# Degree products of a round in four lots of six instead of one lot of 24, and the degree copy behind the last eviction

## The chip, the cores and the metric

The kernel runs on one core of one Trainium2 chip. The metric is the device time of one execution in microseconds; the kernel before takes 1332.59 us (median of 3 runs, 1330.99 to 1334.54). The profile is of one more execution, which took 1327.6 us.

## The reference, cut to what matters

Four graph layers (a three-hop light convolution, a weighted convolution, a mean aggregation, a message network) run one after the other over the same graph of 3125 nodes and 53125 edges, sorted by destination. What the change touches is computed once, ahead of the first layer:

```
# adjacency counts, as a dense matrix
A[s, d] = number of edges from s to d
# first layer and third layer: plain in-degree; second layer: sum of the edge weights + 1
deg  = segment_sum(ones, dst)
deg1 = segment_sum(edge_weight, dst) + 1
x0   = relu(layernorm(x)) * rsqrt(deg)      # what the first product with A takes in
```

## The kernel before, in words

The nodes are cut into 25 chunks of 128 (`NC`), the edges into 416 tiles of 128, taken two at a time as 208 pairs (`PAIRS`). Because the edges are sorted, all edges of a pair end in a window of 20 neighbouring nodes (`PW`). The first stage, the build, makes the matrix `A` (128 x 25 x 3144, half precision) window by window. It has 26 rounds (`ITB`) of 8 pairs (`PS`), and five engines take part, each in its own loop over the rounds, tied by semaphores alone:

- VectorE (`window_hots`, lines 2094 to 2115) makes one-hot tiles: two lane tiles and two small ones a round (`same_as`, L2091) and two tiles for each pair (L2108). Behind pair 2 of a round it makes `hot_d`, 768 wide (L2114), the one-hot of the destinations in a chunk, once GpSimd has made `rel` and once TensorE has used the `hot_d` of the round before (`hot_d_used`).
- TensorE (`windows`) makes a window from two matmuls of 300 or 400 columns (L1552) and one of 25 columns for the edge of the pair (L1557), into one of four PSUM banks of `big`. It may not begin pair k before ScalarE has evicted pair k-4 (`window_kept`).
- ScalarE (`keep_windows`) evicts each window into `A` at a place that it reads from a register (L1345, `A[:, :, bass.ds(bases[k], PW)]`). Each eviction waits for the one before it, as windows overlap. The eight places of a round are loaded from SBUF into registers at its start (`load_nodes`, L1341, whose instruction is at L1024).
- From round 1 on TensorE also makes the degrees of one chunk of 128 nodes: 24 products of 4 columns with 32 columns of weights each (L1566), six for each of four groups of 32 nodes (`SUBS` = 4, `KS` = 6), into bank 0 of `seg`. They stand behind pair 5 (`k == PS - 3`). ScalarE copies the result, 128 x 4, into `deg` behind the eviction of pair 6 (L1349, `k == PS - 2`).
- GpSimd (`chunk_distance`) makes `rel` (L1266) and, once `hot_d_used` has come, copies the four pieces of `w_near` (L1270), which the products of the next round read.

When all 25 chunks have their degrees, VectorE waits for the last copy (`deg_kept`) and works through some twenty short instructions (from L2134) to the first piece of the first layer's input; TensorE then begins the products with `A` (L1628). SyncE starts the reload of `x` and the spill of a part of `A` after the last eviction.

Of the kernel before, what the change touches and what calls it, by code (L numbers as in the profile page):

```python
# [40 lines left out]
PS = 8  # L41
# [6 lines left out]
SUB, KS = 32, 6  # L48
SUBS = P // SUB
# [712 lines left out]
def dense_path(nc, sem, base_row, pair_row, x, src, dst, edge_attr, edge_weight, w1, b1, w2s, w2n, mw1, mb1, mw2, mb2,  # L762
# [3 lines left out]
    with ExitStack() as ctx:  # L766
# [117 lines left out]
        hot_d = cur_h[:, 0:SUB * KD].rearrange("p (v k) -> p v k", k=KD)  # L884
        iota_d = cur_h[:, SUB * KD:2 * SUB * KD].rearrange("p (v u k) -> p v u k", u=SUBS, k=KS)
        w_near = cur_h[:, 2 * SUB * KD:2 * SUB * KD + 4 * KD].bitcast(BF16).rearrange("p (t v) -> p t v", v=4)
# [79 lines left out]
        seg = ctx.enter_context(nc.psum_tensor("seg", [P, 4, 512], F32))  # L966
# [11 lines left out]
        hot_d_ready, hot_d_used = sem("hot_d_ready"), sem("hot_d_used")  # L978
# [22 lines left out]
        ev = sem  # L1001
# [21 lines left out]
        def load_nodes(eng, row, at, n, top):  # L1023
            _, v = nc.values_load_multi_w_load_instructions(  # L1024
                row[0:1, bass.ds(at, n)], engines=[eng.engine], min_val=0, max_val=top,
                skip_runtime_bounds_check_because="node or tile numbers, bounded where they were made")
            return v
# [291 lines left out]
        def on_scalar(act):  # L1319
# [20 lines left out]
            def keep_windows(it, degrees):  # L1340
                bases = load_nodes(act, pair_row, it * PS, PS, N - 1)  # L1341
                for k in range(PS):
                    act.wait_ge(window_built, it * PS + (PS + 1 + k))
                    act.wait_ge(window_kept, it * PS + (k + 4))
                    nc.scalar.copy(A[:, :, bass.ds(bases[k], PW)],  # L1345
                                   big[:, k % 4, 0:PC].rearrange("p (s d) -> p s d", d=PW)).then_inc(window_kept, 1)
                    if degrees and k == PS - 2:
                        act.wait_ge(hot_d_used, it)
                        nc.scalar.copy(deg[:, bass.ds(it - 1, 1), :], seg[:, 0:1, 0:4]).then_inc(ev("deg_kept"), 1)  # L1349

            keep_windows(0, False)
            with act.Fori(1, ITB) as it:
                keep_windows(it, True)
# [139 lines left out]
        def on_tensor(pe):  # L1493
# [23 lines left out]
            for c in range(4):  # L1517
                op = nc.tensor.matmul(banks[7][0:1, P:P + THR], ones[:, :], below[:, c * THR:(c + 1) * THR], start=(c == 0), stop=(c == 3))
            op.then_inc(ev("counts_ps"), 1)
            turn_rows0(4, drel_t, "drel_t")  # L1520
            for c in range(4):
                op = nc.tensor.transpose(banks[6][:, c * P:(c + 1) * P], raw_w[:, c * P:(c + 1) * P], ident[:, :])
# [8 lines left out]
            def pair_window(k):  # L1531

                return big[:, k % 4, 0:PC].rearrange("p (s d) -> p s d", d=PW)
# [5 lines left out]
            def pair_hots(slot, j):  # L1539

                at = NC * FIRST * j
                return hot_r[slot][:, at:at + NC * (SUBWIN[j][1] - SUBWIN[j][0])].rearrange("p (s d) -> p s d", s=NC)

            def windows(it, degrees, odd, first=False):
                for k in range(PS):
                    h = 2 * odd + k // 4
                    if k % 4 == 0:
                        pe.wait_ge(lanes_ready, it * 2 + (k // 4 + 1))
                    pe.wait_ge(hot_r_ready, it * PS + (k + 1))
                    pe.wait_ge(window_kept, it * PS + (k + 1))  # L1550
                    for j, (low, high) in enumerate(SUBWIN):
                        op = nc.tensor.matmul(pair_window(k)[:, :, low:high], hot_l[h][:, :, (2 * k + j) % 8],  # L1552
                                              pair_hots(k % 4 if first else k, j),
                                              start=(j == 0), stop=True, skip_group_check=(j == 1))
                    if k or not first:
                        last = (4 * odd * 4 + 2 * k - 1) % 32
                        op = nc.tensor.matmul(pair_window(k)[:, :, 0], hot_l[last // 8][:, :, last % 8],  # L1557
                                              hot_b[h][:, :, k % 4], start=False, stop=True, skip_group_check=True)
                    op.then_inc(window_built, 1)
                    if degrees and k == PS - 3:  # L1560
                        pe.wait_ge(hot_d_ready, it)
                        pe.wait_ge(ev("w_near_ready"), it * SUBS)
                        pe.wait_ge(ev("deg_kept"), it - 1)
                        for u in range(SUBS):
                            for t in range(u * KS, (u + 1) * KS):
                                op = nc.tensor.matmul(seg[u * SUB:(u + 1) * SUB, 0, 0:4], hot_d[:, :, t], w_near[:, t, :],  # L1566
                                                      start=(t == u * KS), stop=(t == (u + 1) * KS - 1))
                        op.then_inc(hot_d_used, 1)

            windows(0, False, 0, True)  # L1570
            windows(1, True, 1)
            with pe.Fori(1, ITB // 2) as two:
                windows(two * 2, True, 0)
                windows(two * 2 + 1, True, 1)
# [65 lines left out]
            for k in range(ROUNDS):  # L1640
                if k >= 2:
                    pe.wait_ge(ev("conv1_t"), k - 1)
                for c in range(4 * k, min(4 * k + 4, NC)):
                    op = nc.tensor.transpose(seg[0:D, k % 2, (c % 4) * P:(c % 4 + 1) * P], cur[:, c, :], ident[:, :])
# [79 lines left out]
            for half, ks in enumerate((range(0, 3), range(3, ROUNDS))):  # L1724
                pe.wait_ge(ev("h_L3"), half + 1)
                for k in ks:
                    if k >= 4:
                        pe.wait_ge(ev("h_t_L3"), k - 3)
                    for c in range(4 * k, min(4 * k + 4, NC)):
                        op = nc.tensor.transpose(seg[:, k % 4, (c % 4) * P:(c % 4 + 1) * P], h_nb[:, c, :], ident[:, :])  # L1730
                    op.then_inc(ev("h_ps_L3"), 1)
                for k in ks:
# [5 lines left out]
                    for c in range(4 * k, min(4 * k + 4, NC)):  # L1738
                        op = nc.tensor.matmul(big[:, k % 4, (c % 4) * HID:(c % 4 + 1) * HID], h_t[:, c * P:(c + 1) * P], mw1_r, start=True, stop=True)
# [95 lines left out]
            for c in range(4):  # L1835
                op = nc.tensor.matmul(big[:, 0, c * D:(c + 1) * D], y1_t[:, c * P:(c + 1) * P], nw2_sb, start=True, stop=True)
# [686 lines left out]
```

## Time and profile before

| what | us |
|---|---|
| median of 3 runs | 1332.59 |
| the profiled execution | 1327.6 |
| its span (first to last instruction) | 1325.8 |
| TensorE busy / VectorE / ScalarE / GpSimd, of the span | 1006.6 / 830.9 / 452.6 / 592.2 |
| ScalarE evictions of windows (L1345), 208 | 125.4 |
| mean granted TensorE clock, share of full speed | 0.862 |

The build lies between about 25 and 199 us, slices 1 to 6 of the 40 in the page's table; there the granted clock is 0.6 to 0.8 of full speed in tenths (`PEclk 9677778...`). A time in a row is counted from the start of the span. "[0.16 <-X]" behind a row is idle time of the engine ahead of it, and what by the profile ended it; that name is the last event before the start, which need not be what was really waited for. Engine names with a q (ACTq) are the sequencer of that engine, which decodes and hands over; PEld is TensorE's weight load.

### The profile page before, as it was taken

To read this page: it belongs to the slowest core of one execution; us is meant where nothing else is said; L and a number is where in the kernel's file an instruction comes from. 1 tells how busy PE (TensorE), PEld (TensorE's weight loads), DVE (VectorE), ACT (ScalarE), POOL (GpSimd) and SP (SyncE) were. 2 spreads that over 40 slices of the span, in tenths; PEclk is the share of its full clock that TensorE was granted. 3 is DMA by queue.
4 is the path that set the end of the run, shared out by engine and by line. 5 is a ranking of instruction groups with operands and counts; after the bars stand their busy time and mean duration, and the time that the engine had idled before them with its cause. 6 is when DMAs were issued, how large, how long until landed. Compare 5 with 4: busy or idle time off the path is not lost.

```text
span 1325.8 us, 24512 instructions
## 1 busy us (share of the span) xinstructions
PE 1006.6 (76%) x6145; PEld 618.1 (47%) x6145; DVE 830.9 (63%) x2605; ACT 452.6 (34%) x1035; POOL 592.2 (45%) x763
## 2 busy tenths in 40 slices
PE   3788887996667767667696787777787878777685
PEld 2566553553444545445355444434444534444443
DVE  8988877357645556757657554565555555555556
ACT  3677771011434333334013232232232323222232
POOL 6533330000665666654003656555555555555550
PEclk9677778998887788877797899999888998999997
DMA  2000006001111111100523533333333333333331
GB/s 54 2 0 0 0 0 243 1 1 22 24 23 19 20 21 22 21 19 17 168 63 75 138 81 79 76 76 76 77 73 77 75 71 77 75 73 78 72 75 34
DMA packets 145110, 72.80 MB, mean 55 GB/s; under 512 B 111917, under 2 KB 136698, under 8 KB 144922
## 3 DMA queue, kind: packets, MB, share of 16 engines
q1 hardware_dynamic: 127224, 54.98, 16.0%
q0 software_dynamic: 16448, 16.88, 6.9%
q8 instruction: 30, 0.49, 0.2%
q10 hardware_dynamic: 1378, 0.22, 0.1%
q14 instruction: 30, 0.25, 0.1%
HBM read 59.66 MB, written 12.35 MB: 54 GB/s over the span
## 4 chain that ended last, share of the span: by engine, by line
PE 41%; another core or an unknown queue 20%; issue 16%; DVE 12%; ACT 6%; DVEq 2%; POOL 1%; ACTq 1%; DMA 1%; SPq 1%; POOLq 0%
PE seg L1628 10%; PE big L1658 5%; PE big L1552 4%; PE seg L1683 4%; PE seg L1755 3%; PE big L1791 3%; PE seg L1802 2%; ACT A L1345 2%; PE seg L1566 2%; PE big L1781 1%; ACT A L1466 1%; PE seg L1696 1%; ACT A L1472 1%; PE seg L1823 1%
## 5 line engine op out<-in xcount | busy, mean ns | idle before, releaser
L1221 POOL DMA_INDIRECT A<-table,idx x338 | 327.3, 968 | 260.6 <-ACT idx L1317 154.2
L1221 POOL DMA_INDIRECT pair<-table,idx x176 | 176.2, 1001 | 126.8 <-ACT idx L1317 65.0
L1755 PE MATMUL seg<-A 128*128 128x384 f16 (+1 forms) x624 | 137.6, 370 | 44.5 <-issue 19.1
L1466 ACT COPY A<-big 128x512 f32<-128x512 f32 x104 | 61.1, 587 | 249.7 <-remote 156.7
L1345 ACT CAST A<-big 128x500 f32 x208 | 125.4, 603 | 48.0 <-PE big L1557 25.9
L1791 PE MATMUL big<-A 128*128 128x512 f32 x208 | 114.1, 631 | 33.6 <-ACT A L1466 28.3
L2033 DVE COPY A<-seg 128x512 f32<-128x512 f32 x52 | 36.0, 691 | 162.3 <-remote 150.6
L1683 PE MATMUL seg<-A,cur 128*64 128x160 f32 x750 | 94.8, 353 | 46.0 <-issue 45.9
L1397 ACT COPY A<-big 128x500 f32<-128x500 f32 x120 | 66.5, 576 | 181.4 <-remote 113.8
L1755 PEld LDWEIGHTS seg<-A 128*128 128x128 f16 x624 | 60.3, 106 | 140.5 <-issue 91.0
L1658 PE MATMUL big<-A 128*128 128x300 bf16 x480 | 106.1, 367 | 18.8 <-issue 10.4
L1472 ACT ACTIVATE A<-big,A 128x512 f32<-128x512 f32 x104 | 72.1, 694 | 139.0 <-remote 115.5
L1802 PE MATMUL seg<-A 128*64 128x512 f32 x208 | 63.2, 687 | 50.2 <-ACT A L1472 40.6
L1916 DVE TENSOR_SCALAR A<-iota_r,acc_mem,A 128x300 bf16<-128x300 f16 x240 | 74.3, 370 | 39.6 <-remote 32.3
L1683 PEld LDWEIGHTS seg<-A,cur 128*64 128x64 f32 x750 | 61.7, 158 | 75.0 <-issue 71.5
L1628 PE MATMUL seg<-A,acc_mem 128*128 128x512 f16 (+1 forms) x406 | 84.4, 363 | 7.7 <-DVEq L2146 7.7
L2016 DVE TENSOR_TENSOR A<-seg,A 128x448 f32<-128x448 f32 x78 | 48.7, 625 | 56.8 <-PE seg L1758 17.1
L1658 PEld LDWEIGHTS big<-A 128*128 128x128 f16 x480 | 63.4, 151 | 44.6 <-issue 25.1
L1270 POOL COPY cur<-pair 128x24 bf16 x100 | 40.2, 446 | 94.5 <-PE seg L1566 94.5
L2020 DVE TENSOR_REDUCE A<-A 128x64 f32<-128x448 f32 x78 | 72.7, 932 | 4.5
L1781 PE MATMUL big<-ident,A 128*128 128x128 f32 x416 | 67.9, 289 | 5.7 <-issue 3.2
L1371 ACT ACTIVATE acc_mem<-seg 128x512 f32<-128x512 f32 (+1 forms) x28 | 15.2, 544 | 160.0 <-PE seg L1628 159.6
(307 smaller groups left out, 1809.6 us busy)
## 6 DMA issues: line engine op xcount, KB each, us to landing
A<-in_edge_attr_dram SPq DMA_DIRECT2D x103, 128.0 KB
A<-drel_flat SPq DMA_DIRECT2D x104, 126.0 KB
spilled_adjacency<-A SPq DMA_DIRECT2D x1, 7074.0 KB, 21.8
A<-spilled_adjacency SPq DMA_DIRECT2D x6, 1152.0 KB, 11.8
A<-table,idx POOLq DMA_INDIRECT x338
A<-pr_table SPq DMA_DIRECT2D x104, 31.5 KB
pair<-table,idx POOLq DMA_INDIRECT x176
A<-low_flat SPq DMA_DIRECT2D x78, 32.0 KB
```

The source lines that it names most:

```text
L1221: pool.indirect_dma_start(out=row(q, j), out_offset=None, in_=table, in_offset=bass.IndirectOffsetOnAxis(ap=idx[:, q, j:j + 1], axis=0)).t ...
L1345: nc.scalar.copy(A[:, :, bass.ds(bases[k], PW)], big[:, k % 4, 0:PC].rearrange("p (s d) -> p s d", d=PW)).then_inc(window_kept, 1)
L1466: nc.scalar.copy(x_t[:, r, :], big[:, r, :]).then_inc(x_t_ready[r], 1)
L1472: nc.scalar.activation(hid_t[:, q, :], big[:, 2 + r, :], ACT.Relu, bias=mb1_sb).then_inc(hid_ready[r], 1)
L1628: op = nc.tensor.matmul(seg[:, 2 + k % 2, 0:cols], part3(s) if n == 3 else parts[:, s, :, :], A[:, s, 4 * k * P:4 * k * P + cols], start=( ...
L1658: op = nc.tensor.matmul(pair_window(k)[:, :, low:high], hot_l1[:, h, m, :, (2 * k + j) % 8], sub_hots(hot_r1, 2 * (k % 4) + j, high - low) ...
L1683: op = nc.tensor.matmul(seg[side:side + D, 2 + buf, 0:SC], cur[:, s, :], stage1[:, buf, s, :], start=(s < 2), stop=(s >= NC - 2))
L1755: op = nc.tensor.matmul(made[:, 0:held.shape[2] * D], hot_low[:, u, m, :], held[:, k, :, :], start=(m == 0 and k == 0), stop=(m == 3 and k ...
L1781: op = nc.tensor.transpose(big[:, r, j * P:(j + 1) * P], X[:, q, j, :], ident[:, :])
L1791: nc.tensor.matmul(big[:, 2 + r, :], mw1_se, x_t[:, r, :], start=True, stop=False)
L1802: op = nc.tensor.matmul(seg[r * D:(r + 1) * D, 2, :], mw2_sb, hid_t[:, q - 1 + r, :], start=True, stop=True)
L1916: op = dve.tensor_scalar(hot_r1[:, 2 * (k % 4) + j, 0:wide], iota_r[:, 0:wide], key_r[:, bass.ds(t, 1)], scale1[:, bass.ds(t, 1)], ALU.is_ ...
```

## The change

The 24 products of a round are no longer issued together behind pair 5. Six go behind each of the pairs 3, 4, 5 and 6, one group of 32 nodes each, in the same order. The three waits ahead of them stand before the first lot, behind pair 3; `hot_d_used` is raised after the last, behind pair 6. On ScalarE the copy of the degrees and its wait move from behind the eviction of pair 6 to behind that of pair 7, the last of the round.

```diff
@@ keep_windows, ScalarE
-                    if degrees and k == PS - 2:
+                    if degrees and k == PS - 1:
                         act.wait_ge(hot_d_used, it)
                         nc.scalar.copy(deg[:, bass.ds(it - 1, 1), :], seg[:, 0:1, 0:4]).then_inc(ev("deg_kept"), 1)
@@ windows, TensorE
                     op.then_inc(window_built, 1)
-                    if degrees and k == PS - 3:
-                        pe.wait_ge(hot_d_ready, it)
-                        pe.wait_ge(ev("w_near_ready"), it * SUBS)
-                        pe.wait_ge(ev("deg_kept"), it - 1)
-                        for u in range(SUBS):
-                            for t in range(u * KS, (u + 1) * KS):
-                                op = nc.tensor.matmul(seg[u * SUB:(u + 1) * SUB, 0, 0:4], hot_d[:, :, t], w_near[:, t, :],
-                                                      start=(t == u * KS), stop=(t == (u + 1) * KS - 1))
-                        op.then_inc(hot_d_used, 1)
+                    u = k - (PS - 1 - SUBS)
+                    if degrees and 0 <= u < SUBS:
+                        if u == 0:
+                            pe.wait_ge(hot_d_ready, it)
+                            pe.wait_ge(ev("w_near_ready"), it * SUBS)
+                            pe.wait_ge(ev("deg_kept"), it - 1)
+                        for t in range(u * KS, (u + 1) * KS):
+                            op = nc.tensor.matmul(seg[u * SUB:(u + 1) * SUB, 0, 0:4], hot_d[:, :, t], w_near[:, t, :],
+                                                  start=(t == u * KS), stop=(t == (u + 1) * KS - 1))
+                        if u == SUBS - 1:
+                            op.then_inc(hot_d_used, 1)
```

## Rows read from the trace of the kernel before

**Rows 1.** The page, chain that ended last, shares of the span by line.

```profile
PE seg L1628 10%; PE big L1658 5%; PE big L1552 4%; PE seg L1683 4%; PE seg L1755 3%; PE big L1791 3%; PE seg L1802 2%; ACT A L1345 2%; PE seg L1566 2%; PE big L1781 1%; ACT A L1466 1%; PE seg L1696 1%; ACT A L1472 1%; PE seg L1823 1%
```

**Rows 2.** Waits between 50 and 195 us: total us, times, longest us.

```profile
DVE cur L2114 <- PE seg L1566: 19.0, 22, 1.2
PE big L1552 <- ACT A L1345: 17.3, 45, 0.8
ACT A L1345 <- PE big L1557: 16.2, 35, 0.7
```

**Rows 3.** Timeline of ScalarE: start us, us, instruction, count, idle before.

```profile
101.36 0.58 ACT L1345 CAST A<-big 128x500 f32 x1 [0.16 <-ACT A L1345]
102.10 0.67 ACT L1345 CAST A<-big 128x500 f32 x1 [0.16 <-ACT A L1345]
...
104.21 3.34 ACT L1345 CAST A<-big 128x500 f32 x5 [0.69 <-PE big L1557]
107.71 0.58 ACT L1345 CAST A<-big 128x500 f32 x1 [0.16 <-PE big L1557]
108.45 0.58 ACT L1345 CAST A<-big 128x500 f32 x1 [0.16 <-PE big L1557]
...
110.47 3.43 ACT L1345 CAST A<-big 128x500 f32 x5 [0.61 <-ACT A L1345]
...
194.15 3.42 ACT L1345 CAST A<-big 128x500 f32 x5 [0.70 <-PE big L1557]
```

**Rows 4.** Chain of waits from pair 6's eviction into the next round: start us, us, piece.

```profile
95.76 0.08 ACT A L1345
...
95.89 0.04 ACTq L1343
...
96.23 0.15 ACT deg L1349
...
96.50 0.05 ACT A L1345
...
96.57 0.04 ACTq L1352
...
96.88 0.55 ACTq L1024
...
97.77 0.60 ACT A L1345
```

**Rows 5.** Timeline around the lot of 24, in one round and the next.

```profile
100.02 0.96 PEld L1566 LDWEIGHTS seg<-cur 128*32 128x32 f16 x24 [0.34 <-issue]
101.17 0.56 DVE L2114 TENSOR_TENSOR cur<-pair,cur 128x768 f16<-128x768 f16 x1 [1.23 <-PE seg L1566]
101.24 1.60 POOL L1270 COPY cur<-pair 128x24 bf16 x4 [4.41 <-PE seg L1566]
...
101.59 0.25 PE L1557 MATMUL big<-pair,acc_mem 128*128 128x25 f16 x1
...
107.44 0.19 PE L1557 MATMUL big<-xs 128*128 128x25 f16 x1
```

**Rows 6.** Timeline of round 1, from the lot to pair 6's eviction.

```profile
42.46 1.05 PE L1566 MATMUL seg<-cur 128*32 128x4 bf16 x24
43.45 0.80 PE L1552 MATMUL big<-cur,xs 128*128 128x300 f16 x2
44.40 0.59 ACT L1345 CAST A<-big 128x500 f32 x1 [0.92 <-PE big L1557]
```

**Rows 7.** Timeline of the end of the build and the first product with A.

```profile
199.06 0.16 ACT L1349 COPY deg<-seg 128x4 f32 x1
199.25 0.18 DVE L2134 TENSOR_SCALAR pair<-st_c 128x25 f32<-128x25 f32 x1 [4.84 <-ACT deg L1349]
199.34 0.64 ACT L1345 CAST A<-big 128x500 f32 x1
...
205.58 1.44 PE L1628 MATMUL seg<-A,acc_mem 128*128 128x512 f16 x3 [7.68 <-DVEq L2146]
```

## The prediction

> **What bounds the kernel now.** The change lies in the build, so I read the page's chain first, for how much of the span the stage's lines have: L1552, L1345 and L1566 together 8% [rows 1]. The chain puts 2% of the span, some 26 us, on the degree products, as if TensorE were held up by the lot. The second view is the waits of the stage, because a chain takes the last event before a start for its cause. There the engines wait for each other in turn: VectorE behind the lot 19.0 us in 22 rounds, TensorE for evictions 17.3 us, ScalarE "for TensorE" 16.2 us [rows 2]. The third view, ScalarE's timeline, decides which of these is real. The reader is to see the distance from start to start: evictions 5 to 6 of one round 0.74 us (101.36 to 102.10), of the next 0.74 us (107.71 to 108.45) [rows 3]. TensorE ended pair 6 at 101.84 (101.59 and 0.25) in the first and at 107.63 in the second, 0.26 and 0.82 us ahead of its eviction [rows 5]. One margin is three times the other and the distance is the same, so the eviction did not wait for the pair. The 16.2 us are not hunger either: 0.6 to 0.7 us a round of it stands ahead of the first eviction [rows 3], and there the sequencer loads the eight places, 0.55 us long at 96.88, between the last eviction at 96.50 and the next at 97.77 [rows 4]. So ScalarE sets the round: from 104.21 to 110.47 it took 6.26 us, and from 97.77 [rows 4] to 194.15 [rows 3] 15 rounds took 6.43 us each; what lies above 6.26 is evictions of 0.67 in place of 0.58 us. TensorE has the rest as slack, 17.3 us over some 23 rounds [rows 2], 0.75 us a round.
>
> **The change part by part.** The sum is made against the profiled execution, 1327.6 us (span 1325.8); the median of the runs is 5.0 us above it, and I carry the difference over unchanged.
>
> *The lots on TensorE: 0.* The 24 products take 0.98 us (weight loads 0.96, [rows 5]); six take about 0.25 us. The number doesn't change, and the lot behind pair 3 falls into the time in which pair 4 waits for the round's first eviction. What is added are three more entries into such products. The one entry of now shows 0.34 us of idle weight load ahead of it [rows 5]; three of that are 1.0 us a round as the upper end, 0 the lower (six products behind a pair may start as the next pair would). I take 0.3 us, nearer to the lower, because the next pair starts at once behind a lot today. 0.75 us of slack covers that; without the cover a whole 0.3 us would come to 24 x 0.3 = 7 us. What is gained by no longer having 0.98 us ahead of pair 6 is nothing in a round in which pair 6 was early.
>
> The Trainium skill speaks against splitting here: "Perfetto Trace Analysis", Matmul Optimizations, says that TensorE scales its power by use, so that matmuls should run back to back in batches. By it the build's pairs might run at the lower clock more often. The rows show no price of that as long as evictions set the pace; it is weighed as a rival below.
>
> *The three waits, behind pair 3 in place of 5: 0.* In TensorE's queue the pairs 4 to 7 stand behind them. hot_d is made ahead of pair 3's own tiles in VectorE's order, so that wait is always met. w_near: GpSimd needs 1.60 us from the end of the lot [rows 5]; the release now comes behind pair 6, and until pair 3 of the next round there are four pairs and the wait for evictions, at least 2.5 us with evictions 0.68 us apart. About 1 us is left. If that cover were gone, each 0.1 us would cost 2.4 us in 24 rounds. deg_kept: the copy ends some 0.15 us behind the last eviction, for which pair 3 itself had to wait, and a pair lies between. 0.
>
> *hot_d_used later on VectorE: 0.* Pair 6 of 0.4 to 0.6 us now lies ahead of the release, less what the lot behind pair 3 saves. VectorE stood 1.23 us (19.0 us in all) ahead of hot_d, with everything up to pair 2 of the next round made [rows 2, 5]. The wait grows by 0 to 0.65 us, and what stands behind it (tiles of pair 3, lanes, tiles of pair 4) is due four pairs later.
>
> *The copy behind the last eviction: +2.9 us.* This is the part that the change's description doesn't suggest. ScalarE's arithmetic has room for it: today it starts 0.47 us into eviction 6 (95.76 to 96.23) and eviction 7 follows eviction 6 by 0.74 us (to 96.50), as evictions without a copy between them do (0.74) [rows 3, 4]. So its removal there gains 0. At the new place it stands in the sequencer's path: eviction 7, copy, loop end, load of places. By the rows the sequencer hands the copy over and goes on: its next step (L1343) is at 95.89, before the copy starts at 96.23 and 0.13 us behind the eviction's start; behind eviction 7, without a copy, the loop's step is at 0.07 us and begins earlier still [rows 4]. The load waits for no eviction, so the chain from 96.50 to 97.77, 1.27 us, is sequencer time, and the copy's own steps lengthen it. Lower end 0 (they hide). Upper end: the sequencer stands until the copy is done, 0.47 and 0.15 us, +0.6 a round. I take 0.12 us, 0.13 less the 0.01 of a plain step; it is nearest to the row that shows a copy being passed. 24 round changes lie between rounds with a copy and the next: 24 x 0.12 = 2.9 us, between 0 and 15.
>
> The Trainium skill has the same order of things in "Perfetto Trace Analysis", Per-instruction lifecycle: an instruction is pushed into a wait queue, and the sequencer is then ready for the next. By that rule the round change grows by the handing over alone; the trace agrees at 95.89 against 96.23. That a taken branch also goes on past a waiting copy no run here shows yet.
>
> *The last copy: +0.8 us.* VectorE waited 4.84 us for it and began at 199.25, and the chain to the first product with A at 205.58 hangs on that start [rows 7]. The copy moves from 199.06 to 0.5 us behind the last eviction's start, 199.34: 199.84, or +0.8; bounds 0.3 (the copy starts with the eviction) and 1.0 (it waits out its 0.64 us). Nothing hides it.
>
> *Round 1: -0.6 us.* It is the one round in which ScalarE does starve: eviction 6 at 44.40 had 0.92 us of idle time ahead, and pair 6 started at 43.45 right behind a lot begun at 42.46 [rows 6]. With one lot already in the gap ahead of pair 4 and one behind pair 6, about half the 0.98 us goes from in front of it, and eviction 6 comes 0.6 to 0.7 us earlier; then the spacing of 0.74 holds. Bounds 0 and -0.9.
>
> Sum: 2.9 + 0.8 - 0.6 = +3.1 us: 1330.7 for the profiled execution, 1335.7 us as the median.
>
> **The rivals.** (A) *The sequencer stands until the copy is done.* For: no row shows a branch passed with a copy waiting. Against: L1343 at 95.89 [rows 4]. Price 0.6 a round: 24 x 0.6 + 0.8 - 0.6 = +15, 1347.8 us; it decides from the first round change on. (B) *The lot is what the chain says, and spreading it frees the evictions.* For: the chain has it with 2% of the span [rows 1], at least 20 us or 20 rounds of 0.98. One lot hidden ahead of pair 4 and one moved behind pair 6 is 0.5 us each: 20 x 0.5 = 10 us; with +2.9 and +0.8 that is -6.3, 1326.3 us. Against: the equal distances of 0.74 us [rows 3]. (C) *TensorE becomes the bound by the split:* entries at 0.34 us each, 1.0 a round, over 0.75 us of slack, or pairs longer by a lower granted clock. An excess of 0.3 us a round gives 7 us more, 1342.7; slower. (D) *The copy's steps hide under the eviction* and only the ends count: 0.8 - 0.6, 1332.8 us. That the change doesn't do what it says can't be: it is an order of issue alone.
>
> **How the numbers follow.** Forecast 0.64, A 0.09, B 0.06, C 0.06, D 0.15. Least difference told from none: 0.3%, 4.0 us, so the forecast of +3.1 lies inside it, but near. With 1.5 us of scatter in the median either way the forecast gives 0.45 same, 0.18 slower, 0.01 faster; A and C 0.15 slower; B 0.05 faster and 0.01 same; D 0.15 same. Rounded: faster 0.06, same 0.61, slower 0.33. Range 1331 to 1341: the forecast, D, the copy's price up to 0.3 us a round, and the scatter; A, B and the far end of C stay out.
>
> **What would show it.** Right: evictions 4 to 7 of a round still 0.74 us apart or 0.08 more, with the distance over the round change 1.39 to 1.40 where it was 1.27, and a mean round of 6.55 us; round 1 shorter by about 0.6; the last degree copy about 0.5 us behind the last eviction's start, and from it to the first product with A still 6.5 us; VectorE's wait ahead of hot_d longer; GpSimd's copies ended before pair 3. Wrong: a distance over the round change of 1.27 or of 1.8 (D, A); idle time of more than 0.16 us ahead of evictions inside a round (C); evictions closer than 0.68 us (B).

## The result

The changed kernel takes 1342.63 us (median of 4 runs, 1337.05 to 1343.99) against 1331.79 us before (4 runs): ratio 1.0072, interval 1.0037 to 1.0106. On another chip, 12 runs against 25: 1325.96 against 1317.32, ratio 1.0066, interval 1.0034 to 1.0098. Three more runs of the kernel before and one of the early places below, in a slower state of the chip, are left out of the ratios and of the medians here. Ratios and intervals are those on record, which are not always the quotient of the two medians. The changed kernel is slower by 10.8 us, three and a half times the 3.1 us that were forecast, and outside the range of 1331 to 1341 us.

### The profile after

The waits between 50 and 195 us of the changed kernel (total us, times, longest us; the columns of [rows 2]), ScalarE's only:

```profile
ACT A L1345 <- PE big L1557: 23.6, 44, 0.8
```

It was 16.2 us in 35 times [rows 2]. Most of either sum is the 0.7 us ahead of the first eviction of each round, which the prediction already took for sequencer time. ScalarE's timeline shows where the added time stands. One round and its change of the changed kernel:

```profile
100.61 3.44 ACT L1345 CAST A<-big 128x500 f32 x5 [0.69 <-PE big L1557]
104.21 0.58 ACT L1345 CAST A<-big 128x500 f32 x1 [0.16 <-ACT A L1345]
105.38 0.67 ACT L1345 CAST A<-big 128x500 f32 x1 [0.59 <-PE big L1557]
106.65 0.59 ACT L1345 CAST A<-big 128x500 f32 x1 [0.60 <-PE big L1557]
107.13 0.16 ACT L1349 COPY deg<-seg 128x4 f32 x1
108.05 1.27 ACT L1345 CAST A<-big 128x500 f32 x2 [0.76 <-PE big L1557]
```

Two things differ from [rows 3]. Evictions 5, 6 and 7 (104.21, 105.38, 106.65) start 1.17 and 1.27 us apart where 0.74 was the rule: here ScalarE does wait for TensorE, which the text below calls starvation. And from eviction 7 (106.65) to the next round's first (108.05) it is 1.40 us, which was 1.27 [rows 4]. The evictions are as long as before, 0.58 or 0.67.

TensorE's timeline of the same stretch (start us, us, instruction):

```profile
103.91 0.58 PE L1567 MATMUL seg<-cur 128*32 128x4 bf16 x6
104.42 0.81 PE L1552 MATMUL big<-cur,acc_mem 128*128 128x300 f16 x2
105.02 0.25 PE L1557 MATMUL big<-pair,acc_mem 128*128 128x25 f16 x1
105.19 0.56 PE L1567 MATMUL seg<-cur 128*32 128x4 bf16 x6
105.69 0.81 PE L1552 MATMUL big<-xs,acc_mem 128*128 128x300 f16 x2
106.29 0.25 PE L1557 MATMUL big<-pair,acc_mem 128*128 128x25 f16 x1
106.36 0.76 PE L1552 MATMUL big<-acc_mem,xs 128*128 128x300 f16 x2
106.92 0.25 PE L1557 MATMUL big<-xs,acc_mem 128*128 128x25 f16 x1
106.99 0.76 PE L1552 MATMUL big<-acc_mem,xs 128*128 128x300 f16 x2
```

It never idles. From pair to pair it needs 1.27 us where a lot lies between (104.42 to 105.69) and 0.63 where none does (106.36 to 106.99). So a lot of six holds it for about 0.65 us, not 0.25. The same in a round at the higher granted clock:

```profile
90.16 0.52 PE L1552 MATMUL big<-cur,acc_mem 128*128 128x300 f16 x2
...
91.12 0.52 PE L1552 MATMUL big<-xs,acc_mem 128*128 128x300 f16 x2
...
91.51 0.50 PE L1552 MATMUL big<-acc_mem,xs 128*128 128x300 f16 x2
```

Here a pair with a lot takes 0.96 us (90.16 to 91.12) and one without 0.39. The windows view over this round, which has no starvation, and the one above (columns: window, its length, busy us of PE, PEld, DVE, ACT, POOL with counts, granted clock, DMA share, GB/s):

```profile
87.50:94.10 6.60, 5.86 (x51) 4.65 (x51) 6.38 (x26) 4.96 (x9) 2.85 (x11) 1.00 0.00 0
100.60:108.00 7.40, 7.40 (x49) 4.98 (x48) 5.27 (x21) 4.89 (x9) 2.09 (x8) 0.50 0.00 0
```

At granted 1.00, which is 2.4 GHz, the round takes 6.64 us and all pairs are early; at 0.50, 1.2 GHz, TensorE is busy for 7.40 of 7.40 us. This can be worked out from the rows. ScalarE gives a round 5.15 us inside and 1.40 us for its change, 6.55 us. Four pairs with a lot and four without need 4 x 0.96 + 4 x 0.39 = 5.4 us of TensorE at the higher level and 4 x 1.27 + 4 x 0.63 = 7.6 us at the lower, 1.05 us too much. In rounds 2 to 24 of this trace four rounds have 0.50 from their first eviction to their last (6, 10, 14 and 18); they and the round behind each are 1.06 us late on average, and no other round is late by more than 0.05 us.

The end of the stage, TensorE's and ScalarE's timelines of the changed kernel:

```profile
207.40 0.64 ACT L1345 CAST A<-big 128x500 f32 x1 [0.16 <-ACT A L1345]
207.92 0.16 ACT L1349 COPY deg<-seg 128x4 f32 x1
...
214.44 0.59 PE L1630 MATMUL seg<-A,acc_mem 128*128 128x512 f16 x1 [7.77 <-DVEq L2148]
```

The first product with A (line 1630 now) starts at 214.44 where it was 205.58 [rows 7]: +8.86 us of the span's +9.5 (1335.3 against 1325.8). I took each round's eviction starts from the two traces; their differences give 8.8 of the 8.86 us:

| part | us |
|---|---|
| 24 round changes, 1.404 in place of 1.279 | +3.0 |
| last copy 0.52 us behind the last eviction's start, not 0.28 ahead of it | +0.8 |
| round 1, starvation | +0.8 |
| rounds 2 to 24, starvation inside a round, 23 x (5.327 - 5.143) | +4.2 |

### The profile page after: what moved, and what is told of

Its sections match the earlier page's. It is cut to its first block, busy times and chain, and to the rows that moved or that the text cites. A ratio compares the mean times of both kernels' runs of the same rounds, so it can differ in the third digit from the quotient of the medians.

```text
span 1335.3 us, 24512 instructions
## 1 busy us (share of the span) xinstructions
PE 1033.8 (77%) x6145; PEld 644.9 (48%) x6145; DVE 829.2 (62%) x2605; ACT 451.7 (34%) x1035; POOL 595.6 (45%) x763
## 4 chain that ended last, share of the span: by engine, by line
PE 45%; issue 17%; DVE 16%; another core or an unknown queue 15%; ACT 3%; DVEq 2%; ACTq 0%; POOL 0%; DMA 0%; POOLq 0%; SPq 0%
PE seg L1630 10%; PE big L1552 6%; PE big L1660 5%; PE seg L1757 4%; PE seg L1685 4%; PE seg L1567 3%; PE seg L1804 3%; PE big L1793 2%; DVE A L1918 2%; ACT A L1345 2%; PE seg L1825 1%; PE big L1783 1%; DVEq L1024 1%; DVE A L1984 1%
## 5 line engine op out<-in xcount | busy, mean ns | idle before, releaser
L1221 POOL DMA_INDIRECT A<-table,idx x338 | 330.9, 979 | 261.9 <-ACT idx L1317 157.1
L2110 DVE TENSOR_SCALAR acc_mem<-iota_r,acc_mem 128x300 f16<-128x300 f16 (+1 forms) x266 | 69.4, 319 | 0.0
## 6 DMA issues: line engine op xcount, KB each, us to landing
A<-spilled_adjacency SPq DMA_DIRECT2D x6, 1152.0 KB, 11.7
```

The source lines that it names most:

```text
L1221: pool.indirect_dma_start(out=row(q, j), out_offset=None, in_=table, in_offset=bass.IndirectOffsetOnAxis(ap=idx[:, q, j:j + 1], axis=0)).t ...
```

## The experiments

The whole time is a blunt tool: the 6 to 35 runs of one kernel on one chip lay 10 to 19 us apart, and the span behind the first product with A lay between 1095 and 1133 us over all profiles. What moves it stays open: with a mean granted clock of 0.866 behind the first product it was 1132.5 us in the run of the copy alone and 1122.3 us in that of the split alone, on the same chip. So besides the ratio each experiment has the start of the first product with A in its profiled run ("first product"; before 205.58, profiled once), with the eviction times of every round. "The stage" is the span up to that product. In every experiment with a ratio the change of the stage alone gives a ratio inside the interval of the whole, so nothing behind the stage is needed to explain it.

The expectations set three theories against each other. S: the split costs, because each lot holds TensorE. H: the copy at the round change costs all of it. K: the loss is the granted clock in the later stages.

**The copy alone.**

```diff
 # the kernel before
-                    if degrees and k == PS - 2:
+                    if degrees and k == PS - 1:
```

> The kernel before with the second half of the change alone: the degree copy behind the eviction of pair 7, the 24 products still in one lot behind pair 5. Theory S (the split costs: each lot of six holds TensorE about 0.65 us, 1.28 in place of 0.63 us from pair to pair, so it becomes the bound in rounds at the lower clock): here no eviction inside rounds 2 to 24 starts late; the round change is 1.40 in place of 1.27 us, the last copy 0.8 us later, so +3.0 + 0.8 = +3.8 us, 1335.6. Rival H (the copy at the round change is what costs all of it): +10.8 us, 1342.6. Rival K (the loss is the granted clock in the later stages and not in the build): build as by S, but the whole time within 1 us of before or anything up to +10 with the build's end at +3.8.

The first product in TensorE's timeline of this kernel:

```profile
209.27 3.14 PE L1628 MATMUL seg<-A,acc_mem 128*128 128x512 f16 x7 [7.92 <-DVEq L2146]
```

+3.7 us in the stage where S said +3.8. Round changes are 1.405 us, and the time inside rounds 2 to 24 is 5.137 us as before. The median is 1339.11 against 1332.19, ratio 1.0039 (1.0015 to 1.0064); of it the stage explains 1.0028. H falls: the copy is under half of the loss. Two rounds of this trace, 5 and 22, are at granted 0.50 throughout, and neither is late, with the one lot of 24 in it. Round 5 in the windows view and in ScalarE's timeline:

```profile
66.10:72.60 6.50, 5.90 (x48) 3.93 (x47) 5.27 (x21) 4.85 (x9) 2.31 (x8) 0.50 0.00 0
...
69.61 0.65 ACT L1345 CAST A<-big 128x500 f32 x1 [0.16 <-ACT A L1345]
70.43 0.65 ACT L1345 CAST A<-big 128x500 f32 x1 [0.16 <-ACT A L1345]
71.25 0.59 ACT L1345 CAST A<-big 128x500 f32 x1 [0.16 <-ACT A L1345]
```

The idle time ahead of evictions 5 to 7 is 0.16 us, as in the other rounds. So the lower clock alone doesn't starve ScalarE; it takes the four lots as well.

**The split alone.**

```diff
 # the changed kernel
-                    if degrees and k == PS - 1:
+                    if degrees and k == PS - 2:
```

> The changed kernel with the copy put back behind the eviction of pair 6; four lots of six stay. Theory S: round changes of 1.27 again, but evictions 5 to 7 of the rounds at TensorE's lower clock 1.0 to 1.3 us apart; the 3.0 us of round changes go, and part of them comes back as starvation, because ScalarE gives TensorE less slack: +6 to +9 us, about 1339.5. Rival H: +0 to +1 us, 1332.5. Rival K: can't be told from S by the sum, only by the place: the first product with A begins no later than 206.5 us of the span.

The first product in TensorE's timeline of this kernel:

```profile
209.76 2.72 PE L1630 MATMUL seg<-A,acc_mem 128*128 128x512 f16 x6 [7.25 <-DVEq L2148]
```

Round changes are back at 1.278, inside rounds 5.291 us: 3.4 us of starvation, and 0.8 in round 1; stage +4.2, ratio 1.0042 (1.0019 to 1.0064). The two rounds at 0.50 throughout, 2 and 15, are 1.2 and 1.1 us late, and rounds 9 to 12, at 0.50 in part, 0.6 us together. The split alone costs, H falls again, and so does K, which wanted the first product by 206.5. That the two halves sum to 7.9 and not 8.9 is the starvation, which differs from run to run (below).

**Lots of six in mixed order.**

```diff
 # the changed kernel; u is the lot
-                        for t in range(u * KS, (u + 1) * KS):
-                            op = nc.tensor.matmul(seg[u * SUB:(u + 1) * SUB, 0, 0:4], ...
+                        for i in range(u * KS, (u + 1) * KS):
+                            g, t = i % SUBS, i % SUBS * KS + i // SUBS
+                            op = nc.tensor.matmul(seg[g * SUB:(g + 1) * SUB, 0, 0:4], ...
```

> The changed kernel, but the 24 products are issued in the order of their number within a group, so that two products in a row never go to the same 32 columns of the array (every lot of six has products of all four groups). In the changed trace six products of one group follow each other 0.070 us apart, in the trace before two groups ran side by side and 24 products came 0.037 us apart. Theory S with the group as half of the price (S-group): the spacing falls to 0.035 us or less, a lot holds TensorE 0.17 us less, 0.7 us a round; starvation inside rounds goes from about 5 us to about 1, +5 us in all, 1336.8. S-entry (only entering and leaving a lot costs): spacing stays at 0.07, +10.8, 1342.6. Rival H: 1342.6 as well, with nothing changed in TensorE's waits.

Two lots in the timeline of TensorE's weight loads, then the first product:

```profile
101.09 0.21 PEld L1568 LDWEIGHTS seg<-cur 128*32 128x32 f16 x6 [0.34 <-issue]
102.10 0.21 PEld L1568 LDWEIGHTS seg<-cur 128*32 128x32 f16 x6 [0.34 <-issue]
```

and

```profile
209.11 3.15 PE L1631 MATMUL seg<-A,acc_mem 128*128 128x512 f16 x7 [8.23 <-DVEq L2149]
```

Six weight loads take 0.21 us from first to last, in the changed kernel 0.49, and the lots are 1.01 us apart in place of 1.28. From the first product of a lot to the last it is 0.093 us against 0.361, on average 18.5 ns a product against 72. The products of a mixed lot don't come evenly: four, one a group, start within 10 ns, and the second of a group 90 ns behind its first. Inside rounds 5.136 us: no starvation is left from round 2 on; stage +3.5, what the copy alone costs less 0.1 us in round 1 and 0.15 inside the others. Ratio 1.0023 (0.9996 to 1.0051). So with mixed order the four entries, still at four times 0.26 us, fit: the order within the lots was the part that tipped it over. S-entry falls. No round of this trace was at 0.50 from end to end, but rounds 8 and 19 were at 0.53 and 0.52 and not late; by the rows TensorE needs 4 x 1.01 + 4 x 0.63 = 6.56 us at that level, just what a round has.

**One product a lot.**

```diff
 # the changed kernel; 20 of 24 products left out
-                        for t in range(u * KS, (u + 1) * KS):
+                        t = u * KS
...
```

> The changed kernel with one product in each of the four lots in place of six; the other 20 products of a round are left out, so the degrees are incomplete. It measures what entering and leaving alone costs. By the changed trace entering takes 0.177 us from the start of the edge matmul and leaving 0.134 us, against 0.07 us from pair to pair: 0.24 us a lot. Theory S: a pair with a lot behind it takes 0.63 + 0.24 = 0.87 us at the lower clock; no starvation from round 2 on, round 1 a little faster; +3.0 + 0.8 - 0.5 = +3.3 us, 1335.1. S-entry: a pair with a lot still takes over 1.1 us, and the time stays above 1339. Rival H: 1342.6.

The first product in TensorE's timeline of this kernel:

```profile
208.90 2.72 PE L1630 MATMUL seg<-A,acc_mem 128*128 128x512 f16 x6 [8.77 <-DVEq L2148]
```

Stage +3.3, as S had it; no starvation from round 2 on, in rounds 5 and 20 neither, which are at 0.50 throughout. Entering (from the start of the edge matmul) is 0.118 us. Leaving can't be read from the median of 0.238 us here, because TensorE is early and most lots are followed by a wait; where none follows it is 0.160 us, near the 0.139 behind six. Ratio 1.0019 (0.9995 to 1.0043).

**The changed kernel again,** beside the next three.

> The changed kernel as it is, beside the same runs of the kernel before as the next three. In the traces so far the stage ahead of the first product with A (205.58 us before) can be read to 0.1 us, while the rest of the span lay between 1120 and 1133 us with the granted clock. Theory S: first product with A at 214.4 +- 0.5 us again (+8.9), with evictions 5 to 7 starving in about every fourth round, and a median 9 us above before. Rival K (part of the 10.8 us is the later stages' clock, by chance): the first product with A at 214.4, and a median that is less than 7 or more than 12 us above before.

The first product in TensorE's timeline of this kernel:

```profile
211.91 2.72 PE L1630 MATMUL seg<-A,acc_mem 128*128 128x512 f16 x6 [7.47 <-DVEq L2148]
```

Missed, 2.0 us outside its bounds of 0.5: the stage is +6.3, not +8.9. The round changes, the copy and round 1 are the same to 0.1 us; starvation in rounds 2 to 24 is 1.7 us in place of 4.2. It is the part that hangs on which rounds fall to the lower clock: here two (5 and 9) are at 0.50 throughout, 0.86 and 0.81 us late, where the first profile had four. The medians are 8.6 us apart, ratio 1.0066; K, which wanted under 7 or over 12 us, finds no support.

**One lot of 24 in mixed order,** as above, in the kernel before.

> The kernel before, one lot of 24 behind pair 5, with only the order of the products changed so that two in a row never go to the same 32 columns. From the run with mixed lots of six: 18.5 ns a product in place of 37. The lot then takes 23 x 0.0185 = 0.43 us between its first and last product in place of 0.85. Theory S: from round 2 on evictions set the pace, so nothing changes there; round 1 has its eviction 6 0.4 us earlier; first product with A at 205.2, the time -0.4 us, 1331.8, no difference that can be told. Rival: a shorter lot does move the whole stage (the chain view named it in most rounds), 24 x 0.4 = -10 us.

The first product in TensorE's timeline of this kernel:

```profile
204.98 2.29 PE L1628 MATMUL seg<-A,acc_mem 128*128 128x512 f16 x5 [8.04 <-DVEq L2146]
```

The lot takes 0.375 us from first to last product in place of 0.846. The stage gains 0.6 us, 0.5 of it in round 1, and inside rounds it is 5.137 us as before; ratio 0.9982 (0.9953 to 1.0011). Halving what the chain of waits named in so many rounds moved nothing from round 2 on: ScalarE sets the pace.

**Places loaded early.**

```diff
 # the kernel before; the loop over two rounds, other engines unchanged
-                bases = load_nodes(act, pair_row, it * PS, PS, N - 1)
+                bases = list(first)            # four places, loaded by the caller
                 for k in range(PS):
...
+                    if k == 0:
+                        bases += list(places(it, 1))       # places of pairs 4 to 7
+                    if k == 4 and after is not None:
+                        later = places(after, 0)           # first four of the next round
...
-            with act.Fori(1, ITB) as it:
-                keep_windows(it, True)
+            with act.Fori(1, ITB // 2) as two:
+                second = keep_windows(two * 2, True, places(two * 2, 0), two * 2 + 1)
+                keep_windows(two * 2 + 1, True, second)
```

> The kernel before with ScalarE's places loaded in fours and ahead of time: two rounds in one pass of the loop; four places at its start, the other four behind eviction 0, those of the second round behind eviction 4 and 0 of its own. No other engine changes. Theory: ScalarE sets the build's pace, and the round change of 1.28 us is its sequencer's, 0.55 of it the load of eight. The change into every second round falls to 0.74 us as between any two evictions, and the other to about 1.08 (a load of four takes VectorE 0.35 us): 12 x 0.54 + 12 x 0.20 = -8.9 us, of which TensorE at the lower clock (8 x 0.63 + 1.10 = 6.1 us a round against 6.05) takes about 1 back: first product with A at 197.7, the time 1324. Rival (TensorE or VectorE is the bound as soon as ScalarE gains): -3 us at most, with idle time ahead of evictions inside rounds.

ScalarE's timeline over two round changes, then the first product:

```profile
98.52 4.03 ACT L1348 CAST A<-big 128x500 f32 x6
102.71 0.57 ACT L1348 CAST A<-big 128x500 f32 x1 [0.16 <-PE big L1567]
103.45 0.58 ACT L1348 CAST A<-big 128x500 f32 x1 [0.16 <-PE big L1567]
103.92 0.17 ACT L1356 COPY deg<-seg 128x4 f32 x1
104.19 0.67 ACT L1348 CAST A<-big 128x500 f32 x1
105.08 3.44 ACT L1348 CAST A<-big 128x500 f32 x5 [0.22 <-ACT A L1348]
```

and

```profile
193.88 2.72 PE L1638 MATMUL seg<-A,acc_mem 128*128 128x512 f16 x6 [7.67 <-DVEq L2156]
```

The change through the loop's end is 0.89 us (104.19 to 105.08), less than the 1.08 forecast. The load of four takes ScalarE 0.31 us in place of 0.55, which gives 0.24 of the 0.39 us gained; the rest is shorter steps around the load. The other change vanishes into a row of six evictions (98.52) and is 0.71 us. Inside rounds it is 5.139 us as before, so TensorE kept up. The stage is 11.7 us shorter, 3.8 us more than forecast: both changes were shorter, and the 1 us that TensorE was to take back it didn't. Ratio 0.9911 (0.9875 to 0.9948). Only ScalarE's loads and its loop were changed, and the rival, with 3 us at most, falls. So this shows the first reading: ScalarE sets the pace.

**Early places and the mixed lot.**

> The kernel of the places loaded early, with the one lot of 24 in mixed order. Theory: now that ScalarE is faster, the 0.42 us that the mixed lot saves TensorE in a round keeps it out of the way at the lower clock: 0.5 to 1.5 us better than early places alone, first product with A at 196.5, the time 1323. Rival: no difference to early places alone, because VectorE (5.56 us of work a round) or ScalarE stays the bound.

The first product in TensorE's timeline of this kernel:

```profile
193.35 3.15 PE L1638 MATMUL seg<-A,acc_mem 128*128 128x512 f16 x7 [8.04 <-DVEq L2156]
```

That is 3.2 us ahead of the forecast, because early places alone had gained more than forecast. From one start of a round to the next it is 5.933 us against 5.936 without the mixed lot; the 0.5 us between the two kernels is round 1. The rival, no difference to early places alone, holds. It is the fastest kernel of the study, 1304.79 against 1317.32, ratio 0.9897 (0.9855 to 0.9940), with 6 runs and not clearly apart from early places alone.

**Two lots of twelve.**

```diff
 # the changed kernel: groups 0 and 1 behind pair 4, 2 and 3 behind pair 6
-                    u = k - (PS - 1 - SUBS)
+                    u = {PS - 4: 0, PS - 2: 2}.get(k, -1)
...
-                        for t in range(u * KS, (u + 1) * KS):
+                        for t in range(u * KS, (u + 2) * KS):
...
```

> The changed kernel with two lots of twelve, two groups each, behind pairs 4 and 6, in place of four lots of six. Entering and leaving a lot is 0.118 + 0.139 us; two groups side by side give 0.037 us a product, one alone 0.072. Theory S: TensorE's price in a round is 2 x (0.26 + 0.41) = 1.3 us against 1.10 before and 2.47 with four lots, inside its slack: no starvation from round 2 on, evictions 0.74 us apart; round change 1.40 us and the last copy as in the changed kernel. First product with A 3.0 + 0.8 us later than before less some 0.2 in round 1, at 209.2; the time +3.6 us. Rival (any split starves ScalarE, whatever its size): +6 us or more, evictions 5 to 7 over 1 us apart in several rounds.

The first product in TensorE's timeline of this kernel:

```profile
209.93 2.29 PE L1631 MATMUL seg<-A,acc_mem 128*128 128x512 f16 x5 [7.81 <-DVEq L2149]
```

Stage +4.3 where +3.6 was expected: inside rounds 5.149, so 0.1 us of starvation in all; the rest is round 1. A lot of twelve takes 0.52 us from first to last product, not 0.41. Ratio 1.0025 (0.9998 to 1.0051). The rival falls: a split as such doesn't starve ScalarE from round 2 on. No round here was at 0.50 from end to end, the lowest at 0.55, and that one (17) was 0.1 us late.

**The copy last, with early places.**

> The kernel of early places and one mixed lot, with the degree copy behind the eviction of pair 7 as in the change. The copy's price of 0.127 us a round was read as sequencer time in a chain from the last eviction to the next through the loop's end and the load of places. Theory: in the 12 round changes without a loop's end and a load behind them the sequencer now waits for the eviction anyway, so the copy costs 0 there; in the 12 with them (0.89 us, still sequencer) it costs 0.127: 1.5 us, and 0.8 at the end: first product with A at 195.7 against 193.35. Rival (the copy's price is the copy's own time on the engine): 0.127 in all 24 changes, 197.2.

ScalarE's timeline at a change without a loop's end and one with it, in that kernel; and its first product:

```profile
134.74 0.16 ACT L1356 COPY deg<-seg 128x4 f32 x1
134.96 3.48 ACT L1348 CAST A<-big 128x500 f32 x5
...
140.08 0.57 ACT L1348 CAST A<-big 128x500 f32 x1 [0.16 <-ACT A L1348]
140.55 0.17 ACT L1356 COPY deg<-seg 128x4 f32 x1
141.09 3.57 ACT L1348 CAST A<-big 128x500 f32 x5 [0.37 <-ACT A L1348]
```

and

```profile
195.59 2.72 PE L1638 MATMUL seg<-A,acc_mem 128*128 128x512 f16 x6 [8.85 <-DVEq L2156]
```

195.59 for 195.7: the change through the loop's end goes from 0.89 to 1.01 us (140.08 to 141.09), the one without stays at 0.71. The rival (the copy's own time on the engine, 197.2) falls. The price of the copy is sequencer time and is paid only where the sequencer is late. The kernel takes 1324.23 against 1333.34, ratio 0.9932 (0.9908 to 0.9955).

**Windows one column further right.**

```diff
 # the kernel before
-                    nc.scalar.copy(A[:, :, bass.ds(bases[k], PW)],
+                    nc.scalar.copy(A[:, :, bass.ds(bases[k] + 1, PW)],
```

> The kernel before with every window evicted one column further right (the matrix is shifted by one column, so this computes something else). Side question: in rounds 2 to 25 evictions take 0.58 us or 0.65 to 0.67, and the long ones are exactly those 52 whose first column is 5 or 7 modulo 8. If the place alone does it, the long ones are now the 43 pairs whose own first node is 4 or 6 modulo 8, and the stage is 0.8 us shorter. If it is contention with other engines at that point of the stage, the same pairs as before stay long.

Of the 192 evictions of rounds 2 to 25 the long ones (over 0.62 us) are all 22 whose own first node is 4 modulo 8 and all 21 with 6, and no other; before, all 25 with 5 and all 27 with 7. The place alone does it. The other half of the expectation missed, as the first product shows:

```profile
206.29 2.29 PE L1628 MATMUL seg<-A,acc_mem 128*128 128x512 f16 x5 [6.77 <-DVEq L2146]
```

The stage is 0.7 us longer, not 0.8 shorter. The 192 evictions themselves take 0.7 us less (115.1 against 115.8), but the idle time ahead of each inside a round is 0.009 us longer (0.117 or 0.172 in place of 0.108 or 0.163), and all idle time between them 1.3 us. That the added "+ 1" on the register costs it is likely and not shown.

## Why the prediction was wrong

*What bounds the kernel: right.* ScalarE's distances of 0.74 us meant what they were read to mean; the shorter lot gained nothing, the earlier loads 11.7 us.

*The copy behind the last eviction: right.* +2.9 us was said, +3.0 measured (1.279 to 1.404), with the mechanism: the kernel with early places and the copy last came within 0.1 us. The sequencer's own pieces in the round change of the changed kernel, whose copy starts at 107.13 and ends at 107.29, are:

```profile
L1352 ACTq COMPARE_BRANCH  x1: 45/45/45, 106.9 to 106.9; - x1
L1024 ACTq TENSOR_LOAD <-pair_row x1: 548/548/548, 107.2 to 107.2; - x1
```

The branch of the loop's end starts 0.3 us ahead of the copy and the load while the copy still runs, so the sequencer stood for neither. By the Trainium skill, "Perfetto Trace Analysis", Per-instruction lifecycle, the sequencer goes on once an instruction is in the wait queue; the trace agrees, for a branch behind a waiting copy and a load behind a running one too. Rival A, which wanted 1.8 us, falls.

*The last copy: right,* +0.8.

*The lots on TensorE: the step that failed.* "Six take about 0.25 us" was the lot of 24 divided by four, and to it the prediction booked 0.3 us a round for three more entries, 1.0 at most, against 0.75 us of slack; the term came out as 0. From the traces, medians:

| | enter | first to last product | leave | a round |
|---|---|---|---|---|
| one lot of 24 | 0.118 | 0.846 | 0.138 | 1.10 |
| four lots of six | 0.118 | 0.361 | 0.139 | 4 x 0.618 = 2.47 |
| four mixed lots | 0.118 | 0.093 | 0.142 | 4 x 0.353 = 1.41 |

The added 1.37 us a round are 0.77 for three more entries and exits and 0.60 for the products, which don't divide: in the lot of 24, groups of 32 columns ran two side by side, 37 ns a product, and a lot that holds one group runs at 72 ns. At granted 0.50 entering takes 0.178 us and the rest is the same, so a lot of six costs 0.68 us there.

The cover was mis-sized as well. The 0.75 us of slack was a mean over both levels of the clock. At 0.50 seven plain pairs and the one with the lot, 1.74 us from the trace, need 7 x 0.63 + 1.74 = 6.15 us of TensorE against a round of 6.42 before, so 0.3 us was free where it counted. Four lots of six pass that; with mixed order they just fit again, and the starvation was gone. Measured, the term that stood at 0 was +4.2 us in one run of the changed kernel and +1.7 in the other.

The prediction's own sign for rival C came: 0.59 and 0.60 us of idle time ahead of evictions inside a round. C had a chance of 0.06, and in it TensorE becomes the bound by the split. That much is shown, and the clock's part in it by the rounds at 0.50 that are late with four lots of six and not late with one lot of 24. C named the entries or a lower clock, though, and not the products. That its 1342.7 us is the measured time is luck: it has 7 us of starvation, the traces of the changed kernel have 5.6 and 3.1 us, round 1 counted against the booked gain of 0.6, and the medians lie 1.9 us further apart than the stage explains.

The Trainium skill, "Perfetto Trace Analysis", Matmul Optimizations, speaks against taking batches apart, because TensorE scales its power by use. That gave the right side, but the traces don't bear the reason out: the mean granted clock of rounds 2 to 25 was 0.777 against 0.774, that of the whole 0.856 against 0.862. Whether the split makes whole rounds at 0.50 more frequent stays open; the two profiles of the changed kernel had four and two of them in rounds 2 to 24, the kernel before none and the copy alone two.

*Round 1: wrong in sign,* -0.6 said, +0.8 measured, by the same step: it runs at granted 0.50 throughout, so all four lots stand in ScalarE's way, and three of them lie ahead of pair 6.

*The waits moved to pair 3, and hot_d_used: 0, as said.* VectorE's wait ahead of hot_d grew from 19.0 to 25.9 us between 50 and 195 us. Mixed lots of six have the same waits at the same places, and nothing is late there from round 2 on.

*The bound of 4.0 us for a measurable difference* was a little too small: with four runs each the interval reaches 0.35% to either side, 4.6 us.

*Two slips of the working* change nothing. The sum for rival A is 14.6 and not 15 us, 1347.2. And the 1.60 us of GpSimd are counted from the start of its first copy; from the end of the lot it is 1.8 us, which the 2.5 us still cover.

## What to carry to other kernels

Before splitting a batch, price its pieces from a row that has one piece alone: how many products run side by side belongs to the batch, and a mean over it is not the price of a part. Compare the price with the slack at the lower granted clock, not with a mean over both levels. In short lots, small products to different groups of array columns should alternate; in the lot of 24, which was not the bound, it gained 0.6 us only. Where evictions keep an even distance whatever the lead of their producer and a longer one at the loop's end, look at the evicting engine's sequencer: loads of register values and loop ends stand in the same line as the work.

## What the runs showed of the hardware

- Products of 128 x 4 with 32 columns of weights: in a lot of one column group the second starts 90 ns behind the first and each further one 66 to 70 ns behind the one ahead, 72 ns on average. In a lot of 24 that has them group by group two groups overlap, 37 ns a product. With four groups alternating, four start within 10 ns; the average is 18.5 ns in lots of six and 16.3 ns in one lot of 24.
- Entering a lot of six, its products and leaving it take 0.62 us at granted 1.00 and 0.68 at 0.50. A window pair behind it takes 0.36 to 0.39 and 0.63 us.
- ScalarE's eviction of 25 x 20 values to half precision takes 0.58 to 0.60 us, but 0.64 to 0.66 where the first column of the window is 5 modulo 8 and 0.67 to 0.68 where it is 7 (rows of A are 6288 bytes, a whole number of 16): 52 of 52, and 0 of 140 others. Shifted by a column the same pairs were short and others long.
- A register load of 8 values on ScalarE takes 0.55 us and one of 4 0.31 us.
- One more copy behind a round's last eviction moves the sequencer's branch from 0.07 to 0.20 us behind the eviction's start and lengthens the round change by 0.125 us. Where the sequencer isn't late (a round change without a loop's end) it costs nothing.
